# Four graph attention layers: layer 0's transposed rows by DMA, and a table of the exponential loaded ahead of the unit

## The reference

```python
h = jnp.maximum(_layernorm(x, axis=-1), 0.0)
x = x + _L0_gnn_ref(h, adj, L0_gnn_W, L0_gnn_a)
...
x = x + _L1_gnn_ref(h, adj, L1_gnn_W, L1_gnn_a)
...
x = x + _L2_gnn_ref(h, L2_gnn_W, L2_gnn_a, adj, 8192)
...
x = x + _L3_gnn_ref(h, adj, L3_gnn_W, L3_gnn_a)
```

```python
Wh = h @ W
e = (Wh @ a1)[:, None] + (Wh @ a2)[None, :]
e = jnp.where(e >= 0, e, ALPHA * e)
scores = jnp.where(adj > 0, e, NEG_BIG)
attention = jax.nn.softmax(scores, axis=1)
return attention @ Wh
```

## Time and profile before

| | |
|---|---|
| time, median of 3 runs | 3884.77 us (3883.24 to 3884.99) |
| time of the profiled execution | 3884.23 us |
| its span in the profile | 3882.4 us |
| PE busy | 3819.8 us, 98% |
| DVE busy | 3570.3 us, 92% |
| ACT busy | 1187.1 us, 31% |
| DMA queue of SP | 334.41 MB, 27.3% of 16 engines' span |

### The profile page before, as it was taken

How to read it: one execution, slowest core, us unless ns; L and a number is a source line. 1 busy time by engine, 2 the same in 40 slices (tenths; PEclk the granted TensorE clock), 3 DMA queues, 4 the chain that set the end, 5 groups by cost and what they waited for, 6 DMA issues and landing times.

```text
span 3882.4 us, 83778 instructions
## 1 busy us (share of the span) xinstructions
PE 3819.8 (98%) x35555; PEld 3810.9 (98%) x35555; DVE 3570.3 (92%) x7790; ACT 1187.1 (31%) x2492; POOL 17.0 (0%) x107
## 2 busy tenths in 40 slices
PE   7999999999999999999999999999997999999999
PEld 6999999999999999999999999999997999999999
DVE  7888989888899999999999999999997999999998
ACT  6766767676631111111133121121122000000000
POOL 1000000000000000000000000000000000000000
PEclk9999999999999999999999999999998999999999
DMA  7888888888401200000002000000000000000000
GB/s 236 294 289 284 286 282 287 286 279 284 146 18 23 18 20 20 18 20 20 15 15 67 18 20 20 18 20 20 18 17 12 17 12 15 17 12 18 15 18 9
DMA packets 207144, 340.05 MB, mean 88 GB/s; under 512 B 56624, under 2 KB 131504, under 8 KB 206768
## 3 DMA queue, kind: packets, MB, share of 16 engines
q1 hardware_dynamic: 205040, 334.41, 27.3%
q10 hardware_dynamic: 1728, 0.27, 0.0%
HBM read 305.57 MB, written 21.20 MB: 84 GB/s over the span
## 4 chain that ended last, share of the span: by engine, by line
PE 95%; ACT 2%; DVE 2%; DMA 1%; issue 0%; ACTq 0%; SPq 0%; DVEq 0%
PE acc L1240 92%; PE ps_pack L1154 1%; PE ps_wh L1258 1%; ACT vals L1436 1%; DVE q L780 1%; ACT adj_pairs L1341 0%; DMA vals<-in_x_dram 0%; PE ps_wh L1252 0%; DVE mask L753 0%; PE acc L1222 0%; DMA adj_int<-in_adj_dram 0%; PE ps_bc L1198 0%; DMA adj_int<-adj_int 0%; PE acc L1177 0%; ACT xnew L1448 0%
## 5 line engine op out<-in xcount | busy, mean ns | idle before, releaser
L1240 PE MATMUL acc<-vals,q 128*128 128x129 f32 (+1 forms) x32576 | 3671.9, 275 | 5.2 <-DVE q L780 5.1
L1240 PEld LDWEIGHTS acc<-vals,q 128*128 128x128 f32 x32576 | 3653.9, 192 | 6.9 <-issue 5.2
L780 DVE SCALAR_TENSOR_TENSOR q<-rrow,R,mask 128x512 f32<-128x512 f32 x3968 | 2825.7, 745 | 172.0 <-PE acc L1240 28.7
L1341 ACT ACTIVATE adj_pairs<-adj_int,threshold 128x1024 uint8<-128x1024 int32 x512 | 585.3, 1146 | 243.9 <-PE ps_pack L1154 143.1
L753 DVE TENSOR_SCALAR mask<-bits 128x512 uint16<-128x512 uint16 x2048 | 435.9, 285 | 7.4 <-DMA rrow<-rows 4.2
L1448 ACT ACTIVATE xnew<-acc,rec 128x128 f32<-128x128 f32 x244 | 69.3, 366 | 854.6 <-DVE rec L818 760.5
L1455 ACT ACTIVATE e<-xnew 128x512 f32<-128x512 f32 x47 | 29.7, 631 | 405.5 <-DVE xnew L849 317.2
L1468 ACT ACTIVATE e<-xnew,nm,rs 128x128 f32<-128x128 f32 x193 | 79.4, 481 | 214.2 <-DVE nm L625 214.2
L1515 ACT ACTIVATE wh<-ps_wh 128x512 f32<-128x512 f32 x48 | 28.7, 598 | 339.9 <-PE ps_wh L1258 339.8
L1463 ACT ACTIVATE sd<-ve 128x4 f32<-128x4 f32 (+1 forms) x49 | 9.9, 202 | 365.6 <-DVE ve L606 365.5
L849 DVE SCALAR_TENSOR_TENSOR xnew<-mean,none,xnew 128x128 f32<-128x128 f32 x188 | 64.9, 345 | 51.2 <-ACT xnew L1448 51.2
(11 more groups left out here) (228 smaller groups left out, 743.9 us busy)
## 6 DMA issues: line engine op xcount, KB each, us to landing
adj_int<-in_adj_dram SPq DMA_DIRECT2D x512, 512.0 KB, 4.9
rrow<-rows SPq DMA_DIRECT2D x60, 256.0 KB, 3.3
x_between_layers<-xnew SPq DMA_DIRECT2D x32, 256.0 KB, 3.4
xin<-x_between_layers SPq DMA_DIRECT2D x32, 256.0 KB, 2.8
xin<-in_x_dram SPq DMA_DIRECT2D x16, 256.0 KB, 5.2
wh_of_layer<-wh SPq DMA_DIRECT2D x1, 4096.0 KB, 16.7
x_of_layer<-xnew SPq DMA_DIRECT2D x16, 256.0 KB, 2.3
xin<-x_of_layer SPq DMA_DIRECT2D x16, 256.0 KB, 2.8
```

What stands on the lines that cost most here:

```text
L780: nc.vector.scalar_tensor_tensor(q[:, j % RING, :], row, column(R_, t), mask[:, c % 2, j, :], ALU.max, ALU.mult).then_inc(q_ready, 1)
L1240: last = nc.tensor.matmul(to, q[:, j % RING, b * P:(b + 1) * P], vals[:, t, 0:width(g.layer)], start=first, stop=(t == KT - 1 or g.two and ...
L1341: nc.scalar.activation(adj_bytes[:, n % BIN_RING // 2, :, n % 2], adj_int[:, n % ADJ_RING, :], ACT.Sign, bias=threshold[:, 0:1], accum_out ...
```

## The change

`by_dma` now holds in layer 0 as well, for its first 15 groups. So PE's four transposes in 15 of the 16 sweeps of layer 0 go, and so does ACT's copy out of PSUM; in come two copies to halves, a DMA transpose, two copies that join, and one copy that makes the sums. Since the ring of pieces is in use in layer 0, the halves now lie in `hT` and the turned planes in `h`, in all layers. In layer 0 `normalised` moves from i = 23 to i = 21, and SP issues the transpose ahead of piece 25.

The exponential's table for the unit is loaded before the loop, and again at its end for layer 3; its third place, in the middle of the unit, goes.

```diff
-        self.by_dma = not unit and layer in ONE_SWEEP and value < LAST
+        self.by_dma = not unit and layer < 3 and value < LAST
...
-        unread = [after_layer_0[:, a:a + 1] for a in (1920, 1921, 1922)]
+        unread = [after_layer_0[:, a:a + 1] for a in (1920, 1921, 1922, 1923)]
...
-        halves, turned = (flat(adj_int).bitcast(U16)[:, a:a + 2 * W] for a in (1024, 2048))
-        summed_up = flat(adj_int).bitcast(F32)[:, 2048:2048 + W].rearrange("p (b f) -> p b f", b=BLOCKS)
+        halves, turned = flat(hT).bitcast(U16), flat(h).bitcast(U16)
+        summed_up = h
...
             def turn_halves(g):
-                n = (g.layer - 1) * LAST + g.value + 1
+                n = g.layer * LAST + g.value + 1
                 sp.wait_ge(halves_ready, 2 * n)
                 sp.dma_start_transpose(turned.rearrange("p (n r) -> p n r", r=P), halves[:, :]).then_inc(turned_in, 16)
...
                     if before and i == 22:
                         store(before)
+                    if before and i == 25:
+                        turn_halves(before)
                     if before and i == 27:
                         load_next_rows(before)
...
             def join_halves(g):
-                n = (g.layer - 1) * LAST + g.value + 1
+                n = g.layer * LAST + g.value + 1
                 act.wait_ge(turned_in, 16 * n)
...
                 last.then_inc(hT_ready[g.to], 1)
-                if g.layer == 2:
-                    act.wait_ge(hT_ready[g.to], g.value + 1)
+                if g.layer == 1:
+                    return
+
+                act.wait_ge(hT_ready[g.to], g.value + 1)
+                if g.layer == 0:
+                    last = nc.scalar.activation(summed_up[:, :, :], hT[:, :, :], ACT.Copy,
+                                                accum_out=h_sum[:, g.value:g.value + 1])
+                else:
                     for b in range(BLOCKS):
                         last = nc.scalar.activation(summed_up[:, b, :], hT[:, b, :], ACT.Copy, accum_out=h_sum[:, g.tile(b)])
-                    last.then_inc(h_summed, 1)
-                    act.wait_ge(h_summed, g.value + 1)
+                last.then_inc(h_summed, 1)
+                act.wait_ge(h_summed, g.layer // 2 * LAST + g.value + 1)
...
-                act.wait_ge(tr_done[g.to], 1 if g.layer in ONE_SWEEP and not g.unit else g.value + 1)
+                act.wait_ge(tr_done[g.to], g.value + 1 if g.unit else 1)
...
-                    due.append((2 * QP + 7, lambda: normalised(g)))
+                    due.append((2 * QP + 5, lambda: normalised(g)))
...
                     copy_wh(g)
+                if g.layer == 2:
+                    table_of_exp(2)
...
             def outputs_of_unit(u):
-                table_of_exp(2)
                 act.wait_ge(unit_x_in, u.value * 16 + 16)
...
                 copy_wh(u)
+                table_of_exp(3)
```

## The result

| | before | after |
|---|---|---|
| median of 15 runs each | 3884.15 us (3883.0 to 3885.22) | 3876.37 us (3874.44 to 3877.64) |
| profiled execution | 3884.23 us | 3876.38 us |
| its span | 3882.4 us | 3874.5 us |

The ratio is 0.9979, 95% interval 0.9972 to 0.9986: 7.8 us less. Predicted were 3877.2 us (3875.5 to 3880.0). The prediction had drawn its line between faster and the same at 0.2%, and the interval, 0.14% to 0.28%, has that line inside it.

What follows compares the result with a forecast made beforehand. PE was taken as the bound, with 95% of the chain. Terms -6.6 - 0.93 + 0.05 + 0.10 = -7.4 us gave 3876.9 from the profiled execution, 3877.4 from the median; forecast 3877.2, range 3875.5 to 3880.0.

Steps and rivals of the forecast that it cites:

- PE's transposes: Layer 0, groups 0 to 14: four transposes leave PE's stream, 0.44 us a sweep, -6.6 us in all (-6.6 to -9.0).
- more gain: Rival: the transposes cost PE up to their row's 0.60 us, another 2.4 us less, 3874.8 us; chance 0.05.
- cross-check: Layer 0's sweep is 3.98 us longer than layer 1's; four packs make 3.52, leaving 0.46 for PE's transposes.
- Third pack: Layer 0, third chunk: ACT done at 540.6, PE wants the pack at 542.18, so 1.6 us of cover.
- Fourth: Layer 0, fourth chunk: ACT free for the joins from 546.6, with 4.0 us of cover behind them.
- The transfer: Layer 0's DMA transpose lands 6.8 us after 537.1, ahead of the joins; piece 25 0.8 us late under cover; cost 0.
- the pieces starve: Rival: delayed piece 25 and those behind make PE wait 1.9 us at 15 packs, +29 - 7.4, 3906 us; chance 0.07.
- A part of the cover fails: Rival: third or fourth chunk comes some tenths late in many sweeps, half the gain goes, 3880 to 3884; chance 0.12.
- The table: Exponential's table load moved: -0.93 us in the unit, +0.05 ahead of its loop, +0.10 at layer 3's start.
- The sequencer's reads: Reads of the unit's loop bounds run beside the table load; rival: they wait behind it, 3878.6 us, chance 0.05.
- The clock: PE's low clock around 2962 to 2966 could give back 0 to +0.4 us of the table's gain; taken as 0.

Runs made afterwards that it cites:

- doubling: The kernel before, with PE's four transposes of each group of layer 0 done twice: 3890.42 us, ratio 1.0016.
- the run without the move: The changed kernel with ACT's `normalised` left at i = 23 in layer 0, all else as changed: 3880.74 us, ratio 0.999 to the kernel before.

## Why the prediction was right, point by point

**PE's transposes**: -6.6 predicted. The 15 sweeps give -6.59, and doubling gives the same 0.44, so the rival *more gain* is ruled out. (What the prediction's cross-check calls 40 products are 40 matmuls, 20 products; its times are read rightly.) The Trainium skill's page VectorE: DVE Perf Modes, section Rules for kernel authors, advises TensorE for a 128x128 transpose if PSUM will do as destination; the section The three transpose paths has it at 390 ns against 1309 ns by DMA, in bf16. This trace agrees on which is quicker (0.44 us for four blocks on PE, 3.5 us and more by DMA) and not on the choice: PE is the bound here, and a landing that nobody waits for is free.

**Third pack**: cover 1.6 predicted, 1.59 measured. **Fourth**: ACT came to the joins 544.78 - 540.43 = 4.35 us behind the start of the third pack, predicted were 546.6 - 542.18 = 4.4. Behind them stood 0.89 + 2.69, so 3.6 us of the 4.0 predicted; the 0.4 that is missing is about what PE comes sooner itself, without its transposes.

**The transfer** was the step whose size was wrong. Predicted was a landing of 6.8 us, from a store's median and 1.4 on top; measured were 3.5 to 5.8, 4.6 in the median, and 3.1 alone. So piece 25 was hardly late, and ACT waited 0.27 us for it. Cost 0 was right. The rival *the pieces starve* was priced at +29 with all delays added up and carried to every pack; with twice the transfer the loss was 4 us in all. The waits say where the delay went: ACT's waits for the packs, 156 us in all, shrank to 117 and took it up.

**A part of the cover fails**: did not happen, but the run without the move shows that it was two places in ACT's order away, at 3880.74, within the 3880 to 3884 given. Its reason was the thin covers of 1 to 1.6 us, which are the third pack's; more of the loss was at the fourth (1.7 us against 0.8).

**The table**: -0.93 + 0.05 + 0.10 = -0.78 predicted, and -0.78 in the trace, 0.77 with the table alone. The sequencer's reads run beside the load, as two rows had said. The Trainium skill's page ScalarE: Activation LUTs, section What ACT_TABLE_LOAD costs, adds a drain of about 1380 ns; this trace does not show it: the activation behind the 1.28 us load at 2932.24 starts at 2933.53.

**The clock** was taken at 0, with +0.4 as the other end. In single executions the stretch moved from -0.4 to +0.9 against before. The end was too near, and a gain had been left out.

**Missing altogether** was layer 2's wait: PE's instructions were counted for their time, not for where their code is fetched. It gave -0.76 us. The start went the other way by chance (+0.17 and +0.72, with a clock of 0.63 there where it had been 0.76). Sum of the predicted terms -7.4; the ones not predicted (-0.20, -0.76, -0.40, +0.89, -0.09) come to -0.56, and 7.9 is what the spans differ by. The forecast was good to 0.8 us because its large term was exact and the others partly cancelled: what repeats from trace to trace (the sweeps, layer 2's wait, the table) is -8.1 us, more than the 7.4 predicted, and the scatter of one execution (+0.89, -0.40, -0.20) gave 0.3 of it back. That part of the agreement is luck. Of the 0.8 us, 0.6 is the kernel before, whose median was 3884.77 over three runs and 3884.15 over fifteen.

## What to carry to other kernels

Work that leaves the bounding engine pays its full time if each engine that takes it over has a wait there at least as long: list the waits of that engine around the new place, and move the step that starts the chain to the earliest point its input allows. Delays on a queue that feeds an engine with waits of its own should not be added up over the sweeps; take them out of those waits first. Below 1 us of 3900, look at the granted clock at the start and behind each hole before explaining a total, and at more than one trace before giving a stretch to the change. Fill holes of PE with unread products where PE bounds what follows; where DVE does, as at the start of layer 3, it gives nothing.

## What the runs showed of the hardware

- **PE's code comes over the same DMA engines.** A packet of q8 (20 KB by the view's rounding; 4.55 MB in 278 of them is 16 KB each) during a DMA transpose made it land at 4.7 to 4.9 us instead of 3.1, in four kernels; without one it landed at 3.1 in the same place, in seven others. Removing or adding some 60 matmuls 1000 to 2000 us earlier moved it. Why a packet of about 1 us costs some 1.7 us is open.
- **Transposes of the identity keep TensorE's clock up.** With them the granted clock was 1.00 (2.4 GHz) in a window in which it was 0.50 (1.2 GHz) without, and it stayed there through 97 of them in a row, 10.7 us with no other work. The Trainium skill's page TensorE: Matmul & The Clock Gate, section Part 4: PE-mode transpose, says that full clock does not engage for transposes; by these windows it did not fall during them (the trace lists them as MATMUL).
- **A DMA transpose of 256 KB** landed in 3.1 us alone and in 4.6 in the median (3.5 to 5.8) beside loads at 291 GB/s; SP was held 1.23 us by its issue.
